# Linear attention with one tile of TensorE per head instead of a block-diagonal key-value matrix

## What is computed

```python
q = (src @ Wq + bq).reshape(b, s, H, DH)      # H = 16, DH = 64; k and v likewise
Q = jax.nn.elu(q) + 1.0
K = jax.nn.elu(k) + 1.0
KV = jnp.einsum('bshd,bshm->bhdm', K, v)
Z = 1.0 / (jnp.einsum('bshd,bhd->bsh', Q, K.sum(axis=1)) + EPS)
o = jnp.einsum('bshd,bhdm,bsh->bshm', Q, KV, Z).reshape(b, s, H * DH)
attn_out = o @ Wo + bo
```

## Time and profile before

| | us |
|---|---|
| median of 3 runs | 3543.29 |
| lowest, highest | 3523.14, 3543.45 |
| the profiled execution | 3538.98 |
| its span, first to last instruction | 3537.2 |

### The profile page before, as it was taken

How to read it: one execution, slowest core, us unless ns; L and a number is a source line. 1 busy time by engine, 2 the same in 40 slices (tenths; PEclk the granted TensorE clock), 3 DMA queues, 4 the chain that set the end, 5 groups by cost and what they waited for, 6 DMA issues and landing times. The chain is left out here.

```text
span 3537.2 us, 56353 instructions
## 1 busy us (share of the span) xinstructions
PE 2484.3 (70%) x19990; PEld 1783.3 (50%) x19990; DVE 2055.8 (58%) x4732; ACT 1366.1 (39%) x2376; POOL 794.3 (22%) x745
## 2 busy tenths in 40 slices
PE   6999964634675679041599999979234577968994
PEld 3656643421674568021355555549222456966763
DVE  6667664358377124737788888854264894451115
ACT  4444422224011013121388888854115323423332
POOL 0000002200473112723240000002527851105100
PEclk9999986856555579575699999999658798977997
DMA  5000002200074026200100000007201005721000
GB/s 181 1 1 1 1 0 71 42 1 26 0 207 81 3 86 207 64 12 1 36 33 1 1 2 1 1 22 228 77 19 39 9 0 149 223 81 47 25 0 29
DMA packets 156996, 177.64 MB, mean 50 GB/s; under 512 B 55621, under 2 KB 126026, under 8 KB 155882
## 3 DMA queue, kind: packets, MB, share of 16 engines
q1 hardware_dynamic: 135866, 131.59, 13.1%
q0 software_dynamic: 20912, 43.22, 4.0%
HBM read 126.70 MB, written 48.04 MB: 49 GB/s over the span
## 5 line engine op out<-in xcount | busy, mean ns | idle before, releaser
L2442 DVE CUSTOM_DVE_ANT_0 decayed_sd<-decayed_sc,decayed_decay 128x512 f32<-128x512 f32 x512 | 331.7, 686 | 86.0 <-PE decayed_sc L2319 85.8
L2397 ACT ACTIVATE decayed_pr<-decayed_sd,decayed_shift 128x512 f32<-128x512 f32 x512 | 339.0, 713 | 49.2 <-DVE decayed_shift L2449 49.0
L2331 PEld LDWEIGHTS decayed_tr<-all_ident,decayed_pr 128*128 128x128 f32 x2048 | 223.5, 140 | 175.3 <-ACT decayed_pr L2397 101.1
L2331 PE MATMUL decayed_tr<-all_ident,decayed_pr 128*128 128x128 f32 x2048 | 276.8, 278 | 11.1 <-ACT decayed_pt L2404 10.8
L460 PE MATMUL experts_up<-experts_xt,experts_w 128*128 128x256 f32 x1140 | 272.3, 386 | 0.0
L460 PEld LDWEIGHTS experts_up<-experts_xt,experts_w 128*128 128x128 f32 x1140 | 211.6, 194 | 24.8
L386 POOL DMA_INDIRECT rows_in<-L_T,all_slot x128 | 149.2, 1166 | 137.9 <-SPq L2246 82.2
L2456 DVE COPY decayed_pt<-decayed_tr 128x512 f32<-128x512 f32 x256 | 173.3, 685 | 2.6 <-PE decayed_tr L2331 2.6
L437 POOL DMA_DIRECT2D rows_out<-experts_y x121 | 87.4, 722 | 384.9 <-DVE experts_y L522 218.4
L694 PEld LDWEIGHTS moe_down<-moe_w,moe_h 128*128 128x128 f32 x1024 | 131.6, 192 | 56.2 <-issue 55.2
L762 DVE SCALAR_TENSOR_TENSOR all_S<-moe_down,L3b_soft_gate,all_S 128x128 f32 x128 | 42.8, 351 | 191.6 <-PE moe_down L694 191.0
(11 more groups left out here) (512 smaller groups left out, 5554.9 us busy)
## 6 DMA issues: line engine op xcount, KB each, us to landing
experts_w<-in_L_experts SPq DMA_DIRECT2D x78, 384.0 KB, 3.4
experts_w<-in_L_experts SPq DMA_DIRECT2D x43, 579.0 KB, 4.0
experts_tok<-rows_in SPq DMA_DIRECT2D x121, 128.0 KB, 3.4
rows_out<-experts_y POOLq DMA_DIRECT2D x121, 128.0 KB, 3.4
L_b<-bands SPq DMA_DIRECT2D x24, 384.0 KB, 4.8
rows_in<-linear_zero SPq DMA_DIRECT2D x43, 128.0 KB, 1.9
experts_w<-in_L_experts SPq DMA_DIRECT2D x8, 514.0 KB, 3.6
solveb_band<-bands SPq DMA_DIRECT2D x8, 384.0 KB, 4.7
```

The source lines that it names most:

```text
L2331: last = pe.transpose(tr[u % TURNED][:, t * P:(t + 1) * P], pr[:, u % RING, t * P:(t + 1) * P], m.ident[:, :])
L2397: act.activation(pr[:, u % RING, :], sd[:, u % RING, :], ACT.Exp, bias=shift[:, u % RING:u % RING + 1]).then_inc(exp_ready, 1)
L2442: dve.tensor_tensor_reduce(out=sd[:, u % RING, :], in0=sc[h][:, :], in1=decay[:, qt, :], scale=1.0, scalar=-3.0e38, op0=ALU.mult, op1=ALU. ...
```

## The change

Every head gets its own products, in a half of TensorE's array.

```diff
-    VW = P + 1
-    BW = P + 2
+    VW = DH + 1
...
-        V = s.sb("V", [P, TPB, PAIRS, VW])
-        KV = s.sb("KV", [P, PAIRS, BW])
+        V = s.sb("V", [P, TPB, 2 * PAIRS, VW])
+        KV = s.sb("KV", [P, PAIRS, VW])
...
-        inv = s.sb("inv", [P, 2, 2, 2, 2])
+        inv = s.sb("inv", [P, 2, 2, 4])
...
                         for t in range(TPB):
-                            last = pe.matmul(nd[g % 2][:, 0, k * VW:(k + 1) * VW], K[:, t, p * P:(p + 1) * P], V[:, t, p, :],
-                                             start=(t == 0), stop=(t == TPB - 1))
+                            for h in range(2):
+                                last = pe.matmul(nd[g % 2][h * DH:(h + 1) * DH, 0, k * VW:(k + 1) * VW], K[:, t, p * P + h * DH:p * P + (h + 1) * DH],
+                                                 V[:, t, 2 * p + h, :], start=(t == 0), stop=(t == TPB - 1))
...
                                 p = c * 4 + k
-                                last = pe.matmul(nd[c][:, k // 2, k % 2 * BW:(k % 2 + 1) * BW], Q[:, slot, p, t * P:(t + 1) * P], KV[:, p, :],
-                                                 start=True, stop=True)
+                                for h in range(2):
+                                    part = slice(h * DH, (h + 1) * DH)
+                                    last = pe.matmul(nd[c][:, h, k * VW:(k + 1) * VW], Q[part, slot, p, t * P:(t + 1) * P], KV[part, p, :],
+                                                     start=True, stop=True)
...
-                    for k in range(2):
-
-                        part = slice(k * DH, (k + 1) * DH)
-                        src = nd[g % 2][part, 0, 0:2 * VW].rearrange("p (a n) -> p a n", a=2)
-                        act.activation(KV[part, 2 * g:2 * g + 2, part], src[:, :, part], ACT.Copy)
-                        last = act.activation(KV[part, 2 * g:2 * g + 2, P + k:P + k + 1], src[:, :, P:VW], ACT.Copy)
-                    last.then_inc(kv_ready, 1)
+                    act.activation(KV[:, 2 * g:2 * g + 2, :], nd[g % 2][:, 0, 0:2 * VW].rearrange("p (a n) -> p a n", a=2), ACT.Copy).then_inc(kv_ready, 1)
...
-                split_pairs = lambda u: nd[u % 2][:, :, 0:2 * BW].rearrange("p r (a n) -> p r a n", a=2)
+                split_heads = lambda u: nd[u % 2][:, :, 0:4 * VW].rearrange("p h (a n) -> p h a n", a=4)
...
-                    for r in range(2):
-                        last = dve.tensor_tensor(tok[:, t % 2, 4 * c + 2 * r:4 * c + 2 * r + 2, :].rearrange("p a (h n) -> p a h n", h=2),
-                                                 split_pairs(u)[:, r, :, 0:P].rearrange("p a (h n) -> p a h n", h=2),
-                                                 inv[:, u % 2, r].unsqueeze(3).to_broadcast([P, 2, 2, DH]), ALU.mult)
+                    for h in range(2):
+                        last = dve.tensor_tensor(tok[:, t % 2, 4 * c:4 * c + 4, h * DH:(h + 1) * DH], split_heads(u)[:, h, :, 0:DH],
+                                                 inv[:, u % 2, h].unsqueeze(2).to_broadcast([P, 4, DH]), ALU.mult)
...
-            dve.memset(V[:, :, :, P:VW], 1.0).then_inc(preset, 1)
-            dve.memset(KV[:, :, :], 0.0).then_inc(preset, 1)
+            dve.memset(V[:, :, :, DH:VW], 1.0).then_inc(preset, 1)
```

## The result

| | us |
|---|---|
| before, median of 6 runs | 3543.37 |
| after, median of 6 runs | 3564.74 (3558.89 to 3573.0) |
| ratio | 1.007, 95% interval 1.005 to 1.0089 |
| the profiled execution after, its span | 3561.44, 3559.6 |

The change costs some 21 us by the medians, 0.6%; the ratio in the table goes by all the runs. The forecast was 3527, 16 us faster. The time lies in the range that I had given, 3506 to 3573, but by luck: the range reached so high only for another rival, row halves that take turns, and that did not happen. What put the time on the other side of no change was the rival of a falling clock, to which I had given 7%.

A forecast was written before the change was run, and what follows sets the result against it. TensorE was taken to bound the linear phase's rows, with VectorE's search next in line. Rows 0 to 6 (-13.0), row 7 (-2.65) and the start (-0.85) gave -16.5 us: 3527, range 3506 to 3573.

The forecast's parts named there:

- row halves that take turns: Rival for the numerators: row halves take turns, column halves do not; about +30 us, 3573; chance 10%.
- the rival of a falling clock: Rival: tiles fill less of the array, so TensorE's clock falls; three such rows or more, about +35 us net; 7%.
- Key products: In each row, two column halves run at once: 3.7 us in place of 7.3.
- the rival of loads that are not hidden: Rival: weight loads in tiles are not hidden, column halves never overlap load and stream; +10.6 us a row, 3627; 2%.
- Copies, memset, first inverse: Copies of KV 0.39 us less a row; KV's memset gone, start -0.85 once; unit 0's inverse 2.95 earlier.
- Numerators: Eight slots 0.87 us against 0.90; with changes of tiling a unit takes 1.61 against 1.41, +1.1 a row.
- a half-height weight load: Rival for the numerators: a half-height load costs half, slot 0.058 us; about -35 us, 3508 or less; chance 5%.
- The sum: Linear phase: rows 0 to 6 -1.85 us each, row 7 -2.65, start -0.85, in all -16.5.
- The price of the fall: Half the clock over a row's numerators and outputs (18 us busy) costs about +17 us.
- A change of tiling: Between whole-array transposes and tiled numerators: entering costs 0.20 us; changes of tiling make a unit +0.20 longer.

The follow-up runs named there:

- e4_fill: The changed kernel plus one full-array matmul a row (384 moving columns, result unused) ahead of unit 2's wait; 3464.0 us, ratio 0.978.
- e1: The changed kernel with KV widened to 127 columns a pair, so each numerator matmul streams 127 columns instead of 65; 3533.41 us.
- e11: The changed kernel with the search's last step, the sum of the marks, moved behind unit 5 in rows 0 to 6; 3538.95 us.
- e3: The kernel before with only the numerators by head, key products and four copies a group as before; 3568.45 us, ratio 1.0068.

## Why the prediction was wrong, point by point

**Key products: right.** 3.7 us and a tail of 0.2 forecast, 3.95 measured; two column halves do run at once. 128 pairs in 3.95 us are 0.031 each, so the loads are hidden behind matmuls on the same rows. That settles the rival of loads that are not hidden. The Trainium skill says in "TensorE: Matmul & The Clock Gate", section "The mechanism", that a weight load overlaps running matmuls only where it is for other array rows. The same section, a few lines above, allows a load into the background weight buffer as well. This trace does not agree with the narrower rule, for column halves (loads busy 3.81 us beside 3.95 us of matmuls) as the one before did not for the whole array.

**Copies, memset, first inverse: right.** Forecast 4.27 us from the first key matmul (86.58) to the numerators' first load at 90.85, measured 4.33. The inverse stands behind the search, as forecast, at +6.12 (forecast +6.2), and in row 7, without that cover, at +5.55 (forecast +5.4). The key products of row 0 start at 84.18 in place of 86.48. Of these 2.3 us, some 1.3 are the stretch at half clock that the execution before had; the rest, 1.0, is the memset (forecast 0.85).

**Numerators: right at the full clock.** Sixteen loads in 0.97 us; a unit 1.63 against a forecast of 1.61. The two row halves run at once, and a half-height weight load is no shorter (0.97 for sixteen in two halves is the pace of full ones).

**The sum: right where the clock stayed.** In row 7 the last output product comes 25.34 us behind the first key matmul, before 27.94: -2.6, forecast -2.65. In e4_fill, the changed kernel with the clock held, the phase ends 17.2 us early, forecast 16.5. Without the 1.3 us of luck at the start it is 15.9; a row takes 54.26 us there (forecast 54.2).

**The rivals: the failed step.** The sum priced every stage at the full clock. I gave "the clock falls" 7% and wrote against it that half of each unit, and all output products, still fill the array. That is true from the transposes behind unit 2 on. It is not true of the stretch from the numerators' start to there, and in each fallen row of this trace the fall comes at the end of that stretch or within some 1.2 us behind it. Units 0, 1 and 2 follow each other without a transpose between them, and my own sum put a wait there: unit 2's load at 94.05, units 0 and 1 done soon after 92.6. What that stretch does was to be worked out from rows that I had. In the 4.09 us from 88.51 to 92.60, 48 matmuls of 65 columns on half of the array stream no more than 48 / 2 x 65 = 1560 full-array columns; before, the like stretch of 3.34 us (94.55 to 97.89, where the transposes' loads begin) streams 24 x 130 = 3120. Twice the columns in less time. The scan and the solve phase, which I quoted at 0.66 and 0.50, were busy with just such narrow work. I took an average over the stage, where its first units, with the wait among them, bring the fall: filled slots (e1) or a wide matmul in the wait (e4) held the clock in all rows. That these units can let the clock fall is shown; the count of columns does not say which row falls, since rows 1 and 0 of e11 stream the same.

**The price of the fall: right in kind, too high in size.** Forecast +17 us a row where a row's numerators and outputs all run at half. Measured: at half clock are some 13.6 us of the row in rows 0, 2, 4 and 6 and 10.2 in rows 1, 3 and 5. By the last output product behind the first key matmul they cost 32.28 - 26.08 = 6.2 us in row 0 (e4's row as the full-clock one), 4.7 in row 1. Four rows of the one and three of the other are 38.9 us, which turn e4's -17.2 into +21.7; measured +21.3.

## What to carry to other kernels

When an edit narrows what TensorE streams, lay out the stretch around every wait next to it and count full-array columns there, not over the stage: cheaper instructions and a new wait side by side can cost the clock, and then the next stretch (10 to 14 us here) runs at half of it. An edit that "wastes" work, as block-diagonal zeros, padding columns or a spare matmul do, can be the faster one for that reason, so test the halves of such a change apart; here the key products by head alone gain 24 us (3521.39 against 3545.7) and the numerators by head alone lose 23 (3568.45). And before a difference of a per cent is put down to an edit, compare the phases that the edit does not touch: a loop elsewhere may have moved to another place in the code.

## What the runs showed of the hardware that I had not expected

- **32 instructions far ahead of a loop were worth 64 us.** They do next to no work and are spread over the linear phase, which ends some 600 us ahead of the scan. They took the kernel before from 3548.49 to 3477.4; 256 of them did not (3540.16). During the scan 6 packets of instructions arrive instead of 33 or 34. That the code of the loop then lies in a better place, and is not fetched anew each round, is my reading; the packets, TensorE's waits (1.7 instead of 20.1 us on one line) and the clock (0.90 instead of 0.60) are what the traces show.
- **The same code falls in one row and not in the next.** Rows 1, 2, 4 and 5 of e11 stayed at the full clock, rows 0, 3, 6 and 7 did not, and in e3 one of eight fell. The spread of the runs agrees with it (39.5 us in e3 and 31.2 in e11, against 12.4 in e1, 10 runs each), but does not prove it: the kernel before, whose rows did not fall, spread by 28.8 over 25 runs. What exactly decides for one row stays open.
- **A change of tiling costs about 0.2 us on entering, also at 64 rows,** with an idle of 0.17 us at the full clock and 0.33 at half: it goes with TensorE's clock.
